# Convolution taps of three blocks as diagonal matmuls, two more chunks through the f32 product, and a new order of gates and scales in a Mamba/MLP layer on one NeuronCore

## The reference

```
x = x + 0.5 * (layernorm(x) @ W.T + lora/16 + bias)     # W: 4-bit weights, dequantised by groups of 64
x = x + attn(layernorm(x))                               # attn = Mamba2 with residual, then gated MLP
x = x + 0.5 * (the same first sublayer again)

# inside attn
zxbcdt = rmsnorm(h) @ w_in.T          # z 512, xs 128, B 128, C 512, dt 4 columns
xBC    = silu(conv1d(xBC, 4 taps, one channel each) + conv_b)
dt     = softplus(dt + dt_bias);  scan over 16 chunks of 128 tokens, 4 heads, state 128 x 128
y      = (scan + D * xs) * silu(z);  h = h + y @ w_out.T
h      = h + (silu(rms(h) @ gate.T) * (rms(h) @ up.T)) @ down.T      # 1792 inner columns
```

## Time and profile before

| | us |
|---|---|
| median of 3 runs | 804.05 (802.47 to 804.51) |
| profiled execution | 803.85 |
| its span | 802.1 |
| outside the span | 1.75 |
| TensorE busy | 764.0 (95%) |
| VectorE busy | 636.7 (79%) |
| ScalarE busy | 444.2 (55%) |
| GpSimd busy | 336.1 (42%) |
| mean granted clock of TensorE | 0.978 of full |

### The profile page before, as it was taken

The page is one execution under the profiler, slowest core; times in us unless marked ns, Lnnn a source line. Parts: engine busy times, 40 slices in busy tenths (PEclk is TensorE's granted clock), DMA queues, the critical chain, the costliest instruction groups (busy, mean ns, idle before and its releaser), DMA issues.

```text
span 802.1 us, 10670 instructions
## 1 busy us (share of the span) xinstructions
PE 764.0 (95%) x3480; PEld 354.5 (44%) x3480; DVE 636.7 (79%) x1246; ACT 444.2 (55%) x869; POOL 336.1 (42%) x392
## 2 busy tenths in 40 slices
PE   9978799899899989899999799999999999999998
PEld 4333355455445444344444344444444444444443
DVE  7789768777876886786889797787887888757994
ACT  3776567767666666454444545546545645534441
POOL 5513254454444348666523124325225224223674
PEclk9999899999999989899999999999999999999999
DMA  8923432542422111321060263554644644344564
GB/s 300 244 54 74 91 86 67 91 100 47 91 53 54 27 27 40 105 40 40 0 158 14 50 147 55 103 132 73 128 103 80 143 80 80 66 83 75 109 168 131
DMA packets 98166, 72.39 MB, mean 90 GB/s; under 512 B 67984, under 2 KB 75152, under 8 KB 98112
## 3 DMA queue, kind: packets, MB, share of 16 engines
q0 software_dynamic: 17280, 31.46, 22.0%
q1 hardware_dynamic: 80496, 40.20, 19.3%
q10 hardware_dynamic: 336, 0.05, 0.0%
HBM read 20.32 MB, written 4.19 MB: 31 GB/s over the span
## 4 chain that ended last, share of the span: by engine, by line
PE 72%; DVE 14%; ACT 6%; issue 3%; DMA 3%; POOL 1%; SPq 0%; ACTq 0%; DVEq 0%; POOLq 0%
PE PS L1898 61%; PE PS L2021 6%; DMA x_t<-hb 2%; DVE raw L1402 2%; DVE st L1234 1%; DVE stage L1402 1%; PE PS L2003 1%; DVE w_in L1311 1%; PE PS L2011 1%; PE PS L1994 1%; DVE xs L1334 1%; PE PS L1986 1%; ACT pre L846 1%; POOL r L512 1%; ACT th L856 1%
## 5 line engine op out<-in xcount | busy, mean ns | idle before, releaser
L703 POOL DMA_DIRECT2D xs<-x x59 | 51.0, 864 | 151.6 <-ACT x L1107 137.9
L1898 PE MATMUL PS<-h,w_in 128*128 128x512 f16 x480 | 109.0, 379 | 2.5 <-DMA h<-hn_p 2.1
L1898 PE MATMUL PS<-h,x_t 128*128 128x512 f16 x408 | 96.9, 388 | 3.2 <-DVE pre L1741 3.2
L1898 PEld LDWEIGHTS PS<-h,w_in 128*128 128x128 f16 x480 | 46.8, 98 | 68.2 <-issue 16.8
L1898 PE MATMUL PS<-n_T,stage 128*128 128x512 f16 x288 | 71.5, 379 | 0.0
L512 POOL TENSOR_TENSOR r<-mv,mhalf 128x1 f32<-128x1 f32 (+1 forms) x32 | 28.7, 897 | 91.6 <-DVE mv L1238 77.6
L1898 PEld LDWEIGHTS PS<-h,x_t 128*128 128x128 f16 x408 | 40.2, 100 | 54.1 <-issue 9.5
L1107 ACT ACTIVATE x<-PS,d_d 128x512 f32<-128x512 f32 x59 | 40.2, 681 | 38.6 <-PE PS L1898 38.6
L703 POOL DMA_DIRECT2D xs<-n x29 | 25.2, 869 | 72.9 <-ACT n L1107 62.6
L1898 PE MATMUL PS<-pre,stage 128*128 128x512 f16 x192 | 49.3, 379 | 0.0
L1077 ACT ACTIVATE xds<-tm,dgh 128x512 f32<-128x512 f32 x24 | 17.3, 722 | 55.1 <-DVE tm L1829 55.1
(11 more groups left out here) (306 smaller groups left out, 1795.4 us busy)
## 6 DMA issues: line engine op xcount, KB each, us to landing
xs<-x POOLq DMA_DIRECT2D x75, 256.0 KB, 3.3
xs<-n POOLq DMA_DIRECT2D x29, 256.0 KB, 3.2
x_t<-x_in SPq DMA_DIRECT2D x16, 256.0 KB, 3.6
x_t<-hb POOLq DMA_DIRECT2D x16, 256.0 KB, 3.8
out<-x_t SPq DMA_DIRECT2D x16, 256.0 KB, 2.3
raw_gu<-gate_t SPq DMA_DIRECT2D x7, 512.0 KB, 4.4
raw_gu<-up_t SPq DMA_DIRECT2D x7, 512.0 KB, 6.6
...
```

The costliest lines, as they stand in the source:

```text
L703: po.dma_start(chunk_of(xs, c), d_tmps[d % 3], accum_op=ALU.add).then_inc(s_acc[d % 3], 16)
L1898: ins = pe.matmul(out_, lhs(a, b, k), rhs(a, b, k), start=first and n == 0, stop=last and n == len(todo) - 1)
```

## The change

1. `NPC = 3`: blocks 0, 1, 2 of row block 0 are convolved on TensorE. `build_dw` on ScalarE makes 12 diagonal matrices of 128x128 from the identity and the taps; `conv_taps(b)` multiplies the four shifted views of `pre` by them in f32, into banks 4, 6, 7; `conv_post(b)` on ScalarE makes xbc and tanh from PSUM. The taps of these blocks on VectorE go. The diagonals lie in `raw_gu`, so the first load of gate, up and down weights (`load_pair(0)`) moves on SP from the start to behind the loop over chunks 4 to 7.
2. `NF = CH + 2`: chunks 4 and 5 pass through `first_t0`, `tc0`, `first_f`; the f16 route with its DMA_TRANSPOSE begins at chunk 6. Of the 36 `keep_warm` matmuls in front of the prologue 9 stay.
3. conv_w is passed in another layout and loaded by ScalarE's queue. In the prologue ScalarE has `scan_decay(0, 0)` ahead of `hi1(7)`, and `hi0(8)` ahead of `tanh_z(0, 0)`.
4. In the steps VectorE's `gate_y` moves; in step 12 `cut_b` moves behind `gate_up` and `residual2`; `bound_row(0)` moves to the head of step 10; `scales(2)` and `descale(2)` move from unit 2 to the end of unit 1, and `norm(2)` is spread over the head of unit 2 on ScalarE.

```
+        NF = CH + 2
+        NPC = 3
+        B_CONV = (4, 6, 7)
+        dw = raw_gu[:, :, :, :].rearrange("p g k n -> p (g k n)")[:, 0:NPC * NTAP * P].rearrange("p (b t q) -> p b t q", b=NPC, t=NTAP)
...
@@ SyncE
-            load_pair(0)
-            for c in range(CH):
-                next_x(c)
-                t1(c)
-            t0(CH)
-            t0(CH + 1)
+            next_x(0)
+            next_x(1)
+            t1(0)
+            next_x(2)
+            t1(1)
+            next_x(3)
+            t1(2)
+            t1(3)
             for c in range(CH, 2 * CH):
                 t1(c)
                 next_x(c)
                 if c + 2 <= 2 * CH:
                     t0(c + 2)
+            sp_.wait_ge(e_cv, NPC)
+            load_pair(0)
...
@@ ScalarE
+            def build_dw(b):
+                for k in range(NTAP):
+                    last = ac.activation(dw[:, b, k, :], ident[:, :], ACT.Copy, scale=cw[:, b, k:k + 1])
+                last.then_inc(e_dw, 1)
+            def conv_post(b):
+                ac.wait_ge(*taps_done(b))
+                ac.activation(xbc[0][:, b, :], bank(B_CONV[b]), ACT.Identity, scale=d_ih[:, :], bias=cb[:, b:b + 1])
+                if b > 0:
+                    ac.wait_ge(e_xbc, b)
+                ac.activation(th[:, 0, :], bank(B_CONV[b]), ACT.Tanh, scale=d_ih[:, :], bias=cb[:, b:b + 1]).then_inc(e_tanh, 1)
...
@@ VectorE, before the prologue
             lo1(0, 0)
-            ffn_scale()
+            prep0(4, 0)
             x1_stats(2, 2, B_P[0])
             lo1(1, 1)
+            x1_stats(3, 3, B_P[1])
+            ffn_scale()
             w_in_bound()
-            x1_stats(3, 3, B_P[1])
+            prep0(5, 1)
+            lo1(2, 2)
             max_row(1)
-            lo1(2, 2)
...
@@ VectorE, step(c)
+                gate_mid = (j == 2 and a < NCH) or (a >= NCH and c <= 3 * CH and j != 2)
+                if c == 2 * CH + 2:
+                    bound_row(0)
+                if c == 2 * CH + 2 or c >= 3 * CH + 1:
+                    gate_y(c, j)
                 if late:
                     slot_a(i_late, late[0], {1: 3, 2: 12}.get(j))
...
+                    if gate_mid:
+                        gate_y(c, j)
...
-                gate_first = a >= NCH or j == CH - 1
-                if gate_first:
-                    gate_y(c, j)
...
-                    if j == 0:
-                        cut_b()
                     gate_up(0, j)
                 residual2(c, j)
+                if c == 3 * CH:
+                    cut_b()
...
@@ TensorE
+            def conv_taps(b):
+                if b == 0:
+                    pe.wait_ge(e_dw, NPC)
+                pe.wait_ge(e_conv, b + 1)
+                for k in range(NTAP):
+                    last = pe.matmul(bank(B_CONV[b]), dw[:, b, k, :], pre[:, b % 2, k:k + ST], start=k == 0, stop=k == NTAP - 1)
+                last.then_inc(e_cv, 1)
             def prologue():
                 proj(0, 0)
                 proj(0, 1)
                 steps(0)
-                f(4)
+                conv_taps(0)
                 proj(0, 2)
+                conv_taps(1)
                 proj(0, 3)
-                f(5)
+                conv_taps(2)
+                f(6)
                 proj(0, 4)
                 proj(0, 5)
-                f(6)
+                f(7)
                 proj(0, 6)
                 proj(0, 7)
                 csm(0)
-                f(7)
                 proj(0, 8)
                 s1(0)
                 proj(0, 9)
...
```

More of the change, by code:

```diff
@@ L34, in build @@
     DI = w_out_t.shape[0]
-    CONV = conv_w.shape[0]
-    CB = CONV // P
-    NTAP = conv_w.shape[1]
+    CB = conv_b.shape[1]
+    NTAP = conv_w.shape[1] // CB
+    CONV = CB * P
     ZB = DI // P
@@ L968, in prologue @@
                 scan1(0, 0)
+                scan_decay(0, 0)
                 hi1(7, 3)
                 tanh_z(0, 3)
-                scan_decay(0, 0)
                 scan2(0, 0)
@@ L997, in _ @@
             hi1(1, 1)
+            hi0(4, 0)
             w_in_sum(3)
+            tc0(4)
             hi1(2, 2)
+            hi0(5, 1)
             hi1(3, 3)
+            tc0(5)
             ac.wait_ge(e_scale, 2)
@@ L1146, in weight_work @@
                 elif p + 1 < NP:
-                    if n == 2:
+                    if n == 2 and p > 1:
                         norm(p + 1, part)
@@ L1156, in unit @@
                     hi_s(m - 1, 0)
+                if m == 2:
+                    norm(2, 0)
                 copy_p1(m)
@@ L1159, in unit @@
                     hi_s(m - 1, 1)
+                if m == 2:
+                    norm(2, 1)
                 evict(ds[0])
+                if m == 2:
+                    norm(2, 2)
                 tanh_s(m, 0)
@@ L1397, in taps @@
                 ve.wait_ge(e_conv, i * CB + (b + 1))
-                base = (i * CB + b) * 2
+                base = (i * CB + b - NPC) * 2
                 for k in range(NTAP - 1):
@@ L1566, in prologue @@
             def prologue():
-                lo0(4, 0)
+                lo1(4, 0)
                 ffn_lo()
-                prep0(5, 1)
-                taps(0, 0)
-                lo0(5, 1)
+                prep0(7, 3)
                 softplus(0, 0)
@@ L1574, in prologue @@
                 softplus(0, 2)
-                taps(0, 1)
+                lo0(6, 2)
                 silu(0, 0)
                 w_in_lo(2)
-                x1_stats(4, 0, PLAN["f", 4][0])
-                prep0(6, 2)
-                taps(0, 2, 3)
+                lo1(5, 1)
                 silu(0, 1)
-                lo1(4, 0)
-                lo0(6, 2)
-                taps(0, 3, 6)
+                taps(0, 3, 3)
+                x1_stats(6, 2, PLAN["f", 6][0])
+                lo0(7, 3)
                 silu(0, 2)
-                x1_stats(5, 1, PLAN["f", 5][0])
-                prep0(7, 3)
-                taps(0, 4, 9)
+                taps(0, 4, 6)
                 silu(0, 3)
-                lo1(5, 1)
-                lo0(7, 3)
-                taps(0, 5, 12)
-                softplus(0, 15)
-                softplus(0, 16)
-                softplus(0, 17)
+                taps(0, 5, 9)
+                for k in range(12, 18):
+                    softplus(0, k)
+                x1_stats(7, 3, PLAN["f", 7][0])
                 silu(0, 4)
-                x1_stats(6, 2, PLAN["f", 6][0])
                 prep0(8, 0)
@@ L1608, in prologue @@
                 silu_z(0, 2)
-                x1_stats(7, 3, PLAN["f", 7][0])
                 prep0(9, 1)
+                weights(0, 0)
+                scan1(0, 0)
                 silu_z(0, 3)
                 lo1(7, 3)
-                weights(0, 0)
-                scan1(0, 0)
             def step(c):
@@ L1640, in step @@
                     lo0(a + 1, (a + 1) % CH)
-                if c == 2 * CH + 2:
-                    bound_row(0)
-                if not gate_first:
+                if a < NCH and not gate_mid:
                     gate_y(c, j)
@@ L1823, in unit @@
                     t_los(3, 0, 1, 2, 3)
+                    scales(2)
+                    descale(2)
                 if m == NU - 1:
```

138 lines of the change are left out of this document (79 added, 59 removed).

## The result

The changed kernel takes 796.12 us, median of 4 runs (795.61 to 796.33), beside 804.28 for the kernel before: a ratio of 0.9902, 95% interval 0.9884 to 0.9919. So 8.2 us were won where 15.8 were forecast against this median. It is the quickest in TensorE's clock of the four (0.994, the others 0.989).

What follows compares the result with a forecast made beforehand. TensorE was taken to bound the kernel (764.0 of 802.1 us busy), time being won only from its waits and low-clock stretches. 803.85 - 4 - 3.3 - 2.2 - 5.6 - 0.3 = 788.4, given as 788.5; range 779 to 797.

Steps and rivals of the forecast that it cites:

- the main case: Whole kernel: the summed forecast of 788.5 us, with 785 to 792 as its own range and chance 0.50.
- steps 2 and 6: gate_y behind dA ends the wait at w(2); a 2.0 us wait at proj(1, 7) remains; 2 x -1.7 = -3.3 us.
- step 12 at its own place: Step 12: the 3.16 us wait for the gate tile and 2.9 of slow matmuls go; -5.6 us taken.
- the wait for dA stays: Step 10: this wait stays, that of 1.25 for the scale and 0.6 by w(10) go; -2.2 us.
- S for step 14 is ready at 333.7 when TensorE comes to it, with nothing to spare: Behind step 12: S comes just in time for TensorE, so step 12 keeps its -5.6 us.
- A new wait in steps 13 to 15: Sign that the forecast is wrong, named beside a scan start past 103 us.
- The prologue: -4 forecast: Start to scan's first product at 97.3 us: -4 us, bounds -8 and +3, one low stretch of 1.7 charged.
- the prologue gives nothing: Rival, prologue: 7 us more work, one more low stretch, scan at 103, perhaps 2 lost in step 13; 795 us; chance 0.18.
- the rival on the clock through the taps: Prologue, 33 to 73 us: TensorE runs at the lower clock level through the taps; 805.7 us, chance 0.05.
- The clock in the wait that the junk filled: Prologue: removing 27 keep-active matmuls would cost the clock level, 3.4 us or so on two f32 products; 792 us.
- Units: 0.3 to be won by the forecast: Units: scales(2) and norm(2) earlier, VectorE's gating later, same end; -0.3 us, bounds +2 and -5.2.
- 1.1 us won for each work that the adds no longer meet: Units: norm gains by VectorE works no longer beside GpSimd's adds; two such works would make -2.2 us.

Runs made afterwards that it cites:

- e12: The changed kernel run again unaltered: 796.7 us, ratio 0.9926 to the kernel before.
- e3: The changed kernel with the row statistics of step 13 placed between GpSimd's additions of the weights: ratio 0.9892 to the kernel before.
- e6: The kernel before with only cut_b moved behind residual2 of step 12: 802.35 us, ratio 0.9989 to the kernel before.
- e2: The changed kernel with hi0(8) behind tanh_z(0, 0) and tanh(0, 5) on ScalarE: ratio 0.9900 to the kernel before.
- e13: The changed kernel with the edits of e7, e2, e3 and e4, plus cut_decay ahead of lo0(8) and silu_z(0, 1) on VectorE: 785.89 us, ratio 0.9792.
- e4: The changed kernel with norm(2) moved behind tanh_s(2) on ScalarE: ratio 0.9890 to the kernel before.
- e8: The changed kernel with nine junk matmuls added in front of max_turn(1): ratio 0.9910 to the kernel before.
- e7: The changed kernel with ffn_scale and w_in_bound ahead of x1_stats(3) on VectorE: 795.35 us, ratio 0.9917 to the kernel before.

## Why the prediction was wrong, step by step

**Right.** The direction, and the outer range of 779 to 797, but not the 785 to 792 of the main case; w_in_bound late and a wait of 2.9 there (3.05); taps without a wait at 3.44 each; s1(0) at 90.2 (90.64 in e12, where no low stretch lay before it); steps 2 and 6 (the wait goes to projection (1, 7), 1.40 for 2.0, 2.1 won each for 1.7); step 12 at its own place (6.2 for 5.6). In step 10 the wait for dA stays and 1.7 are won for 2.2, but with luck: in four of the twelve profiles with the new order this stretch takes 16.6 to 16.7 us, as long as in the kernel before (16.72), because the w product is at the low level; in eight it takes 15.0 to 15.1.

**The step that failed: "S for step 14 is ready at 333.7 when TensorE comes to it, with nothing to spare"**, and with it the -5.6 that step 12 was to leave. I followed the chain for one step and stopped where it just held. That S was in fact 0.3 us late, but the steps behind it were not counted: TensorE, which was 13.3 us ahead of its old times, ran into engines that were 10 us ahead of theirs, and the four waits (0.28, 1.01, 0.22, 0.88) and what goes with them made the stretch 3.2 us longer. A new wait in steps 13 to 15 was named as a sign of being wrong, and it came. The chain named by e3 goes from GpSimd's additions to the row statistics, ScalarE, VectorE and S; GpSimd's queue was not in my count for these steps at all; its order makes 2.7 of the 3.2. e6 shows that the term is worth 2.9 of its 5.6.

**The prologue: -4 forecast, 1.0 measured.** This term was mis-sized, for the most part by its low stretches. I had charged one of 1.7 us. There is one of 1.4 to 2.8 us before the first projection in six of seven profiles, and one of 1.0 to 2.6 behind the wait of s1(0) in all of them; the wait is 5.5 instead of 3.9, since TensorE comes there about a microsecond earlier than I had it (f(7) hardly waits, 0.23), and S waits 0.7. Added up in e12: s1(0) 0.4 later than forecast, projection 9 slower by 2.6 and S by 0.7 put the scan at 101.4 and not at 97.3, and only 1.7 of that was charged. What the order ahead of s1(0) costs show e2 and e13, where the wait is 4.0 and 1.05. The old prologue varies as much, 101.95 to 104.83 in three profiles, and the one execution that the sum started from was in the middle. This is the rival "the prologue gives nothing", with its 795 and its scan start at 103: what came is near that case, together with the loss behind step 12. Of the rival on the clock through the taps nothing is seen: taps and projections between 46 and 86 us run at full level. The clock in the wait that the junk filled cost 1.4 to 2.8 us in four of seven profiles and nothing in three. From the Trainium skill ("TensorE: Matmul & The Clock Gate", section What's actually happening) I had drawn a steady 3.4; the page itself calls the number of slow matmuls variable from run to run, and the traces agree.

**Units: 0.3 to be won by the forecast, 1.3 lost by the trace (0.6 in six other profiles of this order, whose products behind the wait were less slow).** The delay was in the count (VectorE's next gating work was to wait for ScalarE until 433.7 by the old times; it began at 423.76, which is 433.2 by them), but not who waits for that: VectorE's works behind it free the banks that unit 2's next product writes, and TensorE waited there, until 428.66, and no longer at unit 4. I had GpSimd's adds cost VectorE much the same in either order, and they do: 3.5 us over four instructions in the kernel before (1.11, 1.76, 1.64 and 1.75 for 0.68 each), 3.6 in one instruction now. The rule of the Trainium skill ("GPSIMD Engine Reference", Specifications), names this pair, GpSimd and VectorE instructions with two SBUF inputs, and the traces agree; what I had worked out beside it, 1.1 us won for each work that the adds no longer meet, did not come, because VectorE stood at the first such work until the adds were nearly over. Of the 0.6 us lost between w(15) and unit 1, 0.5 are a wait at 420.09 for ScalarE, which has norm(2, 0) ahead of the copy that TensorE waits for; in e4, where norm stands later, that wait is gone.

**Left open.** What decides in which of two waits TensorE's level falls is not settled: the same program shows both. How much the twelve diagonals on ScalarE, load_pair(0) and t0(9) cost was not tried apart. That e8's junk is the cause of its quick product is consistent with the traces, not shown.

## What to carry to other kernels

When an edit takes a stall of one engine away, follow the others for as many steps as it takes until they have as much lead as the one that gained; where the count says "nothing to spare", charge the difference of the leads, here 3.2 of 6.2 us. Before trusting a gain in a stretch full of waits, list for each in-order queue the instruction that waits at its head and what is ready behind it: e2, e3, e4, e7 and e13 each moved only such an instruction, and together they won 10.8 us (e13 against e12, in two sessions, with ratios of 0.9792 and 0.9926 to the kernel before), more than the change had. And profile a kernel more than once before a single low stretch is put into a sum, or a gain is read from the difference of two traces: of the 2.4 us of e7 and the 2.7 of e4 a good part was the level.
